# Second attention of a fused block: low-half products paired in half-height tiles, with another step order and another place for the row sums

## The reference

```python
def _L1_attn_ref(x, W, b):                      # x: 8 batches, 1024 tokens, 256 wide
    NUM_HEADS = 8                               # d_head = 32
    proj = jnp.einsum('bld,de->ble', x, W) + b  # q, k, v of each head
    qk = jnp.einsum('bhqd,bhkd->bhqk', q, k)
    emb_matrix = sinusoidal_embeddings(length, d_head)
    embeddings = emb_matrix[arange(length)[:, None] - arange(length) + length - 1]
    qe = jnp.einsum('bhqd,qkd->bhqk', q, embeddings)
    weights = softmax((qk + qe) / sqrt(d_head), axis=-1)
    return jnp.einsum('bhqk,bhkd->bhqd', weights, v)
...
x = _L0_conv_ref(x, ...)
t = _to_tokens(x)
t = t + _L1_attn_ref(_ln_t(t), W, b)
t = t + _L1_ffn_ref(_ln_t(t), gate_weight, experts)
```

## Time and profile before

| | |
|---|---|
| median of 3 runs | 2886.41 us |
| profiled execution, its span | 2885.93 us, 2884.0 us |
| PE busy | 2521.5 us, 87% of the span |
| POOL busy | 1982.5 us, 69% |
| DVE busy | 1968.7 us, 68% |
| ACT busy | 1397.2 us, 48% |
| mean granted TensorE clock | 0.941 |

### The profile page before, as it was taken

How to read it: one execution, slowest core, us unless ns; L and a number is a source line. 1 busy time by engine, 2 the same in 40 slices (tenths; PEclk the granted TensorE clock), 3 DMA queues, 4 the chain that set the end, 5 groups by cost and what they waited for, 6 DMA issues and landing times. The chain is left out here.

```text
span 2884.0 us, 47248 instructions
## 1 busy us (share of the span) xinstructions
PE 2521.5 (87%) x18516; PEld 855.1 (30%) x18516; DVE 1968.7 (68%) x3042; ACT 1397.2 (48%) x2548; POOL 1982.5 (69%) x769
## 2 busy tenths in 40 slices
PE   7799999999999999968989999999999999651355
PEld 2463222222222222235542222222222222240144
DVE  3475787887877878457876777777777777277144
ACT  3345555555565555523335555555555555440012
POOL 3114888888888888854447878878878878730763
PEclk8899999999999999989999999999999999875567
DMA  4994112322123221059764222233222230260346
GB/s 78 240 235 128 49 49 58 80 52 52 49 49 83 58 52 49 9 180 302 229 216 93 48 63 48 63 90 69 63 48 63 63 81 16 90 189 9 95 127 238
DMA packets 235262, 277.81 MB, mean 96 GB/s; under 512 B 64550, under 2 KB 170534, under 8 KB 231838
## 3 DMA queue, kind: packets, MB, share of 16 engines
q1 hardware_dynamic: 224544, 249.55, 32.0%
q0 software_dynamic: 6144, 16.85, 1.9%
q10 hardware_dynamic: 4352, 8.39, 0.8%
HBM read 165.03 MB, written 110.47 MB: 96 GB/s over the span
## 5 line engine op out<-in xcount | busy, mean ns | idle before, releaser
L850 POOL TENSOR_TENSOR room_af<-room_af 128x2048 f32<-128x2048 f32 x160 | 725.7, 4535 | 162.9 <-ACT room_af L822 149.1
L1200 POOL TENSOR_TENSOR bias<-bias 128x2048 f32<-128x2048 f32 x160 | 725.0, 4531 | 148.4 <-ACT bias L1172 134.5
L985 DVE TENSOR_REDUCE row_min_kf<-PS 128x1 f32<-128x1024 f32 x512 | 603.7, 1219 | 262.4 <-PE PS L977 260.9
L1172 ACT ACTIVATE bias<-PS 128x512 f32<-128x512 f32 x1024 | 557.2, 596 | 410.3 <-PE PS L1098 408.1
L822 ACT ACTIVATE room_af<-PS 128x512 f32<-128x512 f32 x1024 | 555.9, 594 | 395.6 <-PE PS L744 395.6
L631 DVE CUSTOM_DVE_ANT_0 PS<-PS,bias 128x1024 f32<-128x1024 f32 x512 | 620.0, 1241 | 162.1 <-PE PS L619 142.0
L1098 PE MATMUL PS<-stacks_kf 128*128 128x512 f16 x2048 | 533.4, 383 | 11.7 <-PEq L87 8.4
L737 PE MATMUL PS<-QS_af,KS_af 128*128 128x512 f16 x1024 | 334.2, 387 | 14.3 <-PEq L87 4.5
L1098 PEld LDWEIGHTS PS<-stacks_kf 128*128 128x128 f16 x2048 | 156.3, 97 | 454.5 <-ACT bias L1172 298.3
L770 PE MATMUL PS<-room_af,V_af 128*32 128x512 f32 x2048 | 272.8, 605 | 1.2 <-ACT room_af L822 1.2
L1118 PE MATMUL PS<-bias,V_kf 128*32 128x512 f32 x2048 | 272.7, 604 | 0.0
(11 more groups left out here) (183 smaller groups left out, 2847.3 us busy)
## 6 DMA issues: line engine op xcount, KB each, us to landing
stacks_kf<-query_key_halves SPq DMA_DIRECT2D x112, 256.0 KB, 7.4
query_key_halves<-bias SPq DMA_DIRECT2D x32, 768.0 KB, 4.2
query_key_halves<-room_af SPq DMA_DIRECT2D x32, 512.0 KB
KS_af<-query_key_halves SPq DMA_DIRECT2D x48, 256.0 KB, 4.8
QS_af<-query_key_halves SPq DMA_DIRECT2D x48, 256.0 KB, 6.9
token_rows<-rows_t SPq DMA_DIRECT2D x16, 514.0 KB, 4.3
FT_t<-token_rows SPq DMA_DIRECT2D x16, 514.0 KB
room_af<-in_x SPq DMA_DIRECT2D x16, 512.0 KB, 8.6
```

Source lines behind the costliest of these rows:

```text
L850: nc.gpsimd.tensor_tensor(acc[:, u % 2], so_far, prob[:, n % PR], ALU.add).then_inc(acc_ok, 1)
L985: nc.vector.tensor_reduce(row_min[:, m:m + 1], max_ps[n % len(max_ps)], AX.X, ALU.min).then_inc(max_read, 1)
L1172: nc.scalar.activation(prob[:, n % PR, j, :], score_ps[s % 2], ACT.Exp, scale=-1.0 / (W1S * W1S)).then_inc(exps, 1)
L1200: nc.gpsimd.tensor_tensor(acc[:, u % 2], so_far, prob[:, n % PR], ALU.add).then_inc(acc_ok, 1)
```

## The change

In the second attention:

- **Low products.** The low parts move to a tile of their own, `lows`, with two heads above one another: heads 0 and 2 in partitions 0 to 63, heads 1 and 3 in 64 to 127. A pair of heads is two 128-row products (L1118 of the changed kernel) and then two 64-row products (L1123), in different halves of the array and into different banks. The last of the 64 rows, 63, is the one for the maximum; there was no row free, so the slowest of the 32 table angles is split differently: its table row is centred, and its low part sits in row 127 of QHH, which one small DMA (`load_rest`) writes over what the group load put there, after that load has landed.
- **Score banks** are three instead of two: score s waits for the exponential of s − 3.
- **Row sums.** The products for steps 6 and 7 and for `acc` stand together, 12 matmuls (L1155) in step 1 of the next unit, as one more job in the rotation of the maxima's banks; DVE copies the result to SBUF (L1248) and takes the reciprocals (L1242) there, in steps 2 to 5. POOL's `finish` moves to step 5, behind the fifth addition. In that step the two maxima jobs stand behind the second pair of scores.
- **Loads.** A group is 14 DMAs in place of 11, with the same bytes but for one row of 8 KB. SP waits for the fourth DMA's landing (`high_in`) before it issues `load_rest`. The constant row comes with the table from DRAM, so POOL's six fills go; the tables are 12 DMAs in place of 10.
- **Set-up.** The table gets 34 rows in place of 32, one more DVE operation on one row, and 9 DMAs to DRAM in place of 2. In the token phase ACT's cast of the rotated queries (L371) becomes a copy with a scale from SBUF.

```diff
 def load_group(sp, q, b, g):
-    for r, st, s in ((0, QHH, 0), (1, QHH, 2), (2, QHH, 0), (3, QHH, 2), (0, QL, 1), (1, QL, 3), (0, KH1, 4)):
-        sp.dma_start(stacks[r * D:(r + 1) * D, q % 2, st], src[:, s]).then_inc(stk[q % 2], 16)
+    for r, s in ((0, 0), (1, 2), (2, 0), (3, 2)):
+        sp.dma_start(stacks[r * D:(r + 1) * D, q % 2, QHH], src[:, s]).then_inc(high_in if r == 3 else stk[q % 2], 16)
+    for h in range(2):
+        for first, st, s in ((0, QL, 1), (D, QL, 3), (0, KH1, 4)):
+            first += 2 * D * h
+            sp.dma_start(lows[first:first + D, q % 2, st], src[:, s, h:HG:2]).then_inc(stk[q % 2], 16)
...
+def load_rest(sp, q, b, g, loads):
+    sp.wait_ge(high_in, 16 * loads)
+    sp.dma_start(stacks[4 * D - 1:4 * D, q % 2, QHH], src[D - 1:D, 3]).then_inc(stk[q % 2], 16)
...
-DEN, REC, TAKE, FIN = 2, 3, 1, 4
+DEN, REC, TAKE, FIN = 1, 2, 1, 5
...
 def scores(s):
-    if s >= 2:
-        pe.wait_ge(exps, s - 1)
-    for n, (k_, q_) in enumerate(((KHL, QHH), (KH1, QL))):
-        last = nc.tensor.matmul(score_ps[s % 2], stacks[:, slot, k_, j, ...], stacks[:, slot, q_, j, ...], start=(n == 0), stop=(n == 1))
-    last.then_inc(full, 1)
+    for i in range(2):
+        if s + i >= 3:
+            pe.wait_ge(exps, s + i - 2)
+        nc.tensor.matmul(score_ps[(s + i) % 3], stacks[:, slot, KHL, j + i, ...], stacks[:, slot, QHH, j + i, ...], start=True, stop=False)
+    for i in range(2):
+        half = slice(2 * D * i, 2 * D * (i + 1))
+        nc.tensor.matmul(score_ps[(s + i) % 3], lows[half, slot, KH1, j // 2, ...], lows[half, slot, QL, j // 2, ...],
+                         start=False, stop=True).then_inc(full, 1)
...
+def denominators(n, u):
+    pe.wait_ge(max_read, n - 1)
+    pe.wait_ge(acc_ok, ADDS * (u + 1))
...
 for n in range(NU * KTU + DEN + 1):
     if n < NU * KTU:
         scores(HG * n)
-        scores(HG * n + 1)
+    summed = n >= KTU and n % KTU == DEN
+    if summed:
+        denominators(job_at[(n // KTU - 1, "den")], n // KTU - 1)
+    elif n < NU * KTU:
         maxima(n)
+    if n < NU * KTU:
         scores(HG * n + 2)
-        scores(HG * n + 3)
+        if summed:
+            maxima(n)
     if 1 <= n <= NU * KTU:
         weigh(n - 1)
```

More of the change, by code:

```diff
@@ L28, in build @@
     WS = 64.0
-    W1S = 16.0
     QS = float(D) ** -0.5
@@ L370, in turned_high @@
                             act.wait_ge(added, u * G + g + 1)
-                            nc.scalar.copy(stg[:, u % 2, g, 2, :], rf[:, (u * G + g) % 2, :]).then_inc(r_high, 1)
+                            nc.scalar.activation(stg[:, u % 2, g, 2, :], rf[:, (u * G + g) % 2, :], ACT.Copy,
+                                                 scale=bcol[:, 2 * G:2 * G + 1]).then_inc(r_high, 1)
                         for name in order:
@@ L896, in tile @@
                     return es.enter_context(nc.sbuf_tensor(f"{name}_kf", shape, dt))
-                QHH, KHL, QL, KH1 = range(4)
-                LEAD = 2 * D
-                stacks = tile("stacks", [P, 2, 4, HG, N], F16)
+                QHH, KHL = range(2)
+                QL, KH1 = range(2)
+                LAST = 2 * D - 1
+                stacks = tile("stacks", [P, 2, 2, HG, N], F16)
+                lows = tile("lows", [P, 2, 2, HG // 2, N], F16)
                 V = tile("V", [P, 2, NT, C], F32)
@@ L916, in attention_keys_first @@
                 early_ps = [PS[:, 6:8, :].rearrange("p a n -> p (a n)")]
-                score_ps = [PS[:, 4 + i, :] for i in range(2)]
-                out_ps = PS[:, 6, :]
-                den_ps = PS[:, 7, :]
+                score_ps = [PS[:, 4 + i, :] for i in range(3)]
+                out_ps = PS[:, 7, :]
                 UB = G * NC
@@ L961, in move_maxima @@
                     for j in range(HG):
-                        sp.dma_start(stacks[LEAD:LEAD + 1, slot, QL, j, first:first + CH].rearrange("p (t n) -> p t n", n=P),
+                        row = j % 2 * 2 * D + LAST
+                        sp.dma_start(lows[row:row + 1, slot, QL, j // 2, first:first + CH].rearrange("p (t n) -> p t n", n=P),
                                      max_row[j * TT:(j + 1) * TT, u % 2, :]).then_inc(m_in[u % 2], 16)
@@ L1067, in _ @@
                                     load_values(sp, bb + 1, (b0 + bb + 1) % B)
+                                if u % NC == 0 and q + 1 < NG:
+                                    load_rest(sp, q + 1, (b0 + (q + 1) // G) % B, (q + 1) % G, q + 1)
                                 if u + 1 < NU:
@@ L1289, in _ @@
                                      ).then_inc(x_in, 16)
[L1290 to L1292 removed]
+                    sp.wait_ge(e_low, 2)
+                    for t, pieces in enumerate((((0, D, 0),), ((0, D - 1, 1), (D, D + 1, 1)), ((0, D - 1, 1), (D - 1, D, 0)),
+                                                ((0, D - 1, 0), (D, D + 1, 1)), ((0, D - 1, 0), (D + 1, D + 2, 0)))):
+                        row = 0
+                        for first_, last_, s in pieces:
+                            sp.dma_start(edram[t, row:row + last_ - first_, :], e_p[first_:last_, s, :]).then_inc(e_out, 16)
+                            row += last_ - first_
                     sp.wait_ge(tab_half, NR)
```

129 lines of the change are left out of this document (70 added, 59 removed).

## The result

| | before | after |
|---|---|---|
| median (4 runs each) | 2885.63 us | 2858.05 us (2855.66 to 2859.75) |
| profiled execution, its span | 2885.93, 2884.0 us | 2855.66, 2853.8 us |
| one unit of the second attention | 30.69 us | 29.71 us |
| second attention, first score to last `finish` | 991.7 us | 962.7 us |
| mean granted TensorE clock | 0.941 | 0.941 |

The ratio is 0.9907, 95% interval [0.9894, 0.9919]. Forecast were 2857 (2838 to 2876) and faster. The medians differ by 27.6 us, the two profiled executions by 30.3; the four runs of the changed kernel lie 4 us apart, so the forecast is met to within that spread, and the last microsecond of the agreement says nothing.

What follows compares the result with a forecast made beforehand. PE was taken as the bound, busy 30.64 of a unit's 30.69 us. Units -31.6, last unit +1.5 and second token phase +1 sum to -29.1 against 2885.93: 2856.8, forecast as 2857 us, range 2838 to 2876.

Steps and rivals of the forecast that it cites:

- The low pair runs side by side: Second attention: a pair's two 64-row products take one slot; the rival, that they don't, had chance 0.06 and 2932 us.
- Ordinary step 3.32: Second attention, steps 0, 3, 4, 5, 7: 3.47 us falls to 3.32, set by the exponentials, not PE's sum of 3.15.
- the point where the sign turns: Second attention: the change turns slower if a low pair costs 0.11 us more than a slot.
- Step 1, 2, 6: Second attention: 5.89 us with all row sums, 3.48 with DVE late, 3.69 with a job waiting for DVE.
- Unit: Second attention: a unit takes 29.66 us against 30.68, 1.02 less; 31 units give -31.6 us.
- The first unit: Start of the second attention: no term of its own, counted among the 31 units at 1.02 us less each.
- The last unit: End of the second attention: no maxima, so no saving; POOL sets the end, together +1.5 us.
- POOL: Second attention: five additions take 23.2 us, leaving 1.5 to spare; rival that a transfer or POOL is late: chance 0.10.
- maxima's transfers: Between units of the second attention: at most 5.2 us needed, 5.6 available, at least 0.4 to spare, so no cost.
- Group loads: Second attention: more issues and one 8 KB row cost 2 to 3 us of a margin of 4, so nothing.
- Second token phase: Before the second attention: SP stands some 6 us for a landing before `load_rest`; +1 us, bounds 0 and +6.
- the +1: Second token phase: the 1 us added for SP's wait before `load_rest`, with 0 and +6 as bounds.

Runs made afterwards that it cites:

- e1: Changed kernel with both low products of a pair in the same half of the low tile; ratio 1.0149 to the kernel before.
- e8: Changed kernel with each low product over all 128 rows, so a pair's two heads come one after the other; ratio 1.0061 to the kernel before.
- e3: Changed kernel with every exponential on 256 of the 512 columns, PE's products unchanged; ratio 0.9806 to the kernel before.
- e4: Changed kernel with one of step 1's two maxima jobs before the row sums, their copy between DVE's two reductions; ratio 0.988 to the kernel before.
- e5: Changed kernel with step 6's second maxima job behind the second pair of scores; ratio 0.9888 to the kernel before.
- e6: Changed kernel with both splits of maxima jobs, in steps 1 and 6; 2852.46 us, ratio 0.9868 to the kernel before.
- e7: Changed kernel with one or two extra scratch memsets on POOL behind step 3's addition; ratios 0.9925 and 1.0087 to the kernel before.
- e9: Changed kernel with the maxima moved between units by eight transfers of half the size, not four; ratio 0.9928 to the kernel before.
- e0: Changed kernel run again unchanged; median 2860.3 us, ratio 0.989 to the kernel before.
- e7, 1: Changed kernel with one extra scratch memset of 1024 columns on POOL behind step 3's addition; ratio 0.9925 to the kernel before.
- e7, 4: Changed kernel with two extra scratch memsets of 1900 columns on POOL behind step 3's addition; ratio 1.0087 to the kernel before.

## Why the prediction was right

**The low pair runs side by side**: right, shown by the 0.23 of a pair, by e1 and by e8. The whole gain hangs on it.

**Ordinary step 3.32**: 3.34. Its reason, the exponential that frees a bank and not PE's sum, is shown by e3. Taking the wait from the first attention's rows, where order and banks are the same, was good to 0.02: the exponential starts a little later (0.50 for 0.47), and the wait is 0.19 for 0.17. Five steps and 31 units make it 3 us. The prediction did carry two values for this wait, 3.32-3.15 = 0.17 in the step and 0.14 from its count of starts; the smaller one went into the point where the sign turns and into the expectations of e1 and e3, and was the one that missed.

What a change of shape costs can be told apart from the wait in e3, where the wait is gone and the step is 3.15: eight slots of 0.215 are 1.72, the values up to the next high product take 1.00 with the change behind them, and the other four changes share the 0.43 that is left, 0.11 each. Another tile of the same shape costs nothing (the two maxima jobs). The Trainium skill, "TensorEngine Tiling (Array Packing)", section "Key Properties", says that changing the mode, and not only the tile, drains the engine; the trace agrees. If the drain of about 128 cycles of "TensorE: Matmul & The Clock Gate" of the Trainium skill, section "Step-by-step: what each phase is for", were its price, 0.05 us, the step would be 2.86, an estimate; the measurement decides.

**Step 1, 2, 6**: 5.86, 3.49, 3.69 against 5.89, 3.48, 3.69. Their reasons, DVE late with two reductions in step 2, and the transpose's result that blocks a maxima job in step 6, are shown by e4 and e5: each step loses its wait, and only it, when one job moves (in e4 together with the copy of the sums on DVE).

**Unit**: 29.71 against 29.66; 31 units, -30.4 and not -31.6.

**The first unit** was counted like the others. From the first score to the last unit's step 0 the changed kernel is 31.95 us faster (951.02 to 919.07), 1.55 more than 30.4. The first unit itself takes 30.41 before and 27.77 after (step 0 to step 0): 2.64 less where an ordinary unit saves 0.98 (the other 30 save 29.3). It has no sums of a predecessor. After, that takes 5.86-3.34 = 2.52 out of its step 1; before, it takes 0.86 out of step 0 and 0.86 out of step 2, for its own step 7 has its part of the sums: 0.80 more saved, which the prediction never took off. Its steps 2 and 3 are also shorter than in other units, 3.25 each (1515.99 to 1519.24 to 1522.49): 0.33. The other 0.5 lies in its steps 0 and 1, whose first 2.6 us run at a granted clock of 0.50 in both kernels, and was not traced.

**The last unit** took 2.9 more, not 1.5. From step 0 to POOL's first addition it is 9.0 (9.1 was worked out). The rest is the last sums, which wait for POOL:

```profile
2436.52 23.18 POOL L1229 TENSOR_TENSOR bias<-bias 128x2048 f32<-128x2048 f32 x5 [3.47 <-ACT bias L1199]
...
2459.84 4.29 PE L1155 MATMUL PS<-bias,den_w_kf 128*32 128x512 f32 x24 [2.27 <-POOL bias L1229]
...
2468.42 1.26 POOL L1212 TENSOR_TENSOR oN_kf<-oS_kf,bias 128x512 f32<-128x512 f32 x1 [6.08 <-DVE bias L1242]
```

They take 4.29 us where those of a whole unit take 2.78: +1.5, a term that the prediction didn't have. The clock fell in them in this execution; in e4, e5 and e6, where the same sums follow the same wait, it doesn't (last section). It and the first unit's 1.55 cancel by chance.

**POOL** 1.67 to spare, 1.5 worked out; **maxima's transfers** about 2.1 to spare where at least 0.4 was claimed: both right on the safe side, shown by e7 and e9. **Group loads** (15 DMAs each, the one of `load_rest` counted, against 11) are never late: no step 6 is longer than 3.69.

**Second token phase**: whether the +1 is there stays open. SP does stand, as the rows of its queue show:

```profile
1317.52 0.43 SPq L966 DMA_DIRECT2D V_kf<-values  x1
1322.82 0.64 SPq L963 DMA_DIRECT2D stacks_kf<-query_key_halves  x1
```

4.9 us pass between them (about 6 were expected). What it costs depends on where the phase is taken to begin. From the last score product of the first attention (L737, L741) to the first score of the second it is 288.9 before and 288.2 after. But the last sums of the first attention stand between, and they differ; before, then after:

```profile
1224.54 4.36 PE L782 MATMUL PS<-room_af,den_w_af 128*32 128x512 f32 x24 [1.06 <-POOL room_af L850]
```

```profile
1224.25 2.78 PE L786 MATMUL PS<-room_af,den_w_af 128*32 128x512 f32 x24 [1.06 <-POOL room_af L854]
```

From their end it is 280.5 before and 281.4 after, 0.9 longer. The traces of the experiments, with the same token phase as after, have 281.2 to 284.4 there, and there is only one trace of the kernel before. Set-up (with the first token phase) and the tail moved by -0.95 and -0.2, the first attention up to its last score product by +0.7. In the traces of the experiments, which share this code, these stages take 252.3 to 257.7, 369.7 to 388.1 and 965.6 to 966.8 us, so such moves say nothing. Sum of the span: -0.95+0.7-0.7-29.0-0.2 = -30.2, against -29.1 predicted.

## What to carry to other kernels

Price a new order of products by a stage of the same kernel that already has it: the wait for the bank came with it, to 0.02 us. Half-height products pay only side by side in different halves (1.25 us a unit here, of which the rest of the change gives 0.27 back), and the wait that they uncover is in the engine that frees their banks. When work moves past a loop's border, write down for the first and the last pass which parts of it each still has: here the first unit saved 1.7 us more than counted, half of it for this reason. And where the engine stands idle before a stretch of work, as before the last sums, one trace of it can be off by 1.5 us by a clock that falls in some executions and not in others.

## What the runs showed of the hardware

The last sums begin after PE has stood idle 2.27 us. The busy times by stretch, of the changed kernel, show the granted clock falling in them, from full (2.4 GHz) to half (1.2 GHz):

```profile
2455.00:2457.50 2.50, 2.33 (x19) 0.35 (x18) 0.00 (x0) 1.14 (x3) 2.36 (x2) 1.00 0.01 3
2459.80:2462.00 2.20, 2.16 (x16) 0.77 (x20) 0.00 (x0) 0.00 (x0) 2.06 (x2) 0.77 0.03 7
2462.00:2464.00 2.00, 2.00 (x12) 0.27 (x4) 0.00 (x0) 0.00 (x0) 0.35 (x1) 0.50 0.00 0
```

It is no fixed price: in e0, the same kernel, they take 4.13 after 2.28 of waiting, in e9 4.48 after 2.30, but in e4, e5, e6 and e8, after 2.25 to 2.30, only 2.78. After longer waits they were long each time: 4.48 after 2.99 (e7, 1), 4.48 after 3.50 (e3), 4.88 after 5.33 (e7, 4). Before, the last sums are a third as long, start after 1.85 of waiting and take 1.06 at full clock. The first attention's last sums, shown above, have it too: with 1.06 us of idle time before them in every trace, they take 4.36 in the kernel before (clock 0.50 in their first half), 4.45 in e3 and 4.23 in e7, 4, and 2.78 in the other ten. What decides it stays open; it moves single traces by 1.5 us at each of the two places.

Two smaller ones: a first 64-row product behind a 128-row one starts 0.54 behind the pair's start, a 128-row one 0.44 (e8), the price of a shape by itself; and where two products share a half, one of the other half starts 0.01 us behind the first (e1), ahead of the low product that stood before it in the list; it saves nothing there, since the half used twice has four products to do either way.
